# Transposing the attention probabilities with SyncE's DMA queue in place of TensorE, in a fused layer on 8 cores

## Chip, cores and metric

The program runs on 8 NeuronCores of one Trainium2 chip, all with the same instructions and each with its own slice of the tokens; no core waits for another. The metric is the device time in microseconds of the slowest core.

## What is computed

The input is two sequences of 4096 tokens of width 2048. The layer normalizes them, runs local attention (32 heads of 64, blocks of 64 tokens that see their neighbours, and 16 "sink" keys per head) and a feed-forward net of 8192 beside it, and adds their gated product:

```python
xn = _layernorm(x, axis=-1)
# attention: q, k (rotated), v from xn; per head and block of queries
s_band = einsum(Qb, Kband) * scale            # masked to |distance| <= 64
s_sink = einsum(Qb, sinks) * scale
p = softmax(concatenate([s_sink, s_band], -1))
O = p[..., :S] @ sinks + p[..., S:] @ Vband
s = O @ Wo.T + bo
g = silu((silu(gate) * up) @ w_down.T)        # gate, up from xn
x = x + s * g
```

## The kernel before

Each core owns 1024 tokens and 64 more on either side, 1152 in all. The program has four stages, with a barrier between them: the layer norm with its transposes (up to about 150 us), the merged stage of projections and attention (about 150 to 1250 us), the feed-forward net with the output projection (to about 2900 us), and the last transposes with the residual. Only the merged stage is touched.

**The merged stage.** It has 17 steps. Step c (0 to 15) makes the projections of chunk c, which is two heads: two units of q and three of k (two of 512 tokens, one of 128), 16 matmuls each (L513), and where c is even nine units of v for the next four heads (L526 to L529). In the same step the attention of the chunk before, c-1, is done: eight *pairs* j, one for each 128 queries. Units and pairs alternate in the queue of every engine: unit, pair, unit, pair, until one kind runs out. So an odd step has five units and eight pairs, an even step (2 to 14) fourteen units and eight pairs, and step 16 has eight pairs alone. In an odd step the last three or four pairs stand with no unit between them; this text calls them the *tail*. Pairs 16 to 23 belong to step 3 and pairs 24 to 31 to step 4.

**A pair.** For each of two heads (A and B), 128 queries against 256 keys and 16 sinks:

1. `sc` on TensorE: masks, sinks and keys into `psA`, `psB` (L545 to L548).
2. `mx` on VectorE: the two row maxima, scaled (L632 to L636).
3. `ex` on ScalarE: the exponentials into `pA_bf`, `pB_bf`, 128x272 bf16 (L693, L696).
4. `nm` on VectorE: reciprocal of the sums and two scalings in place (L641 to L646). L646 is its last instruction.
5. `tp` on TensorE: six transposes into `ps_tp` (L557 to L562), four of 128x128 for the keys and two for the 16 sinks.
6. `ev` on VectorE: four copies, two of 128x256 to `pt_sb` (L651, L652) and two of 16x128 to `pts_sb` (L653, L654).
7. `av` on TensorE: the product with v, six matmuls into `ps_o` (L577 to L583).
8. `oe` on ScalarE: two copies to `o_buf` (L663, L665).

**What sets the order.** The lists `tsched`, `vsched` and `ssched` are built once (L403 to L437) and every engine follows its list in order. For pair j TensorE has sc(j), tp(j-1), av(j-2); VectorE mx(j), nm(j), ev(j-1); ScalarE ex(j), oe(j-2). What is left at a step's end, av of the last but one pair, tp and av of the last, is put ahead of the next step's units on TensorE. `pA_bf`, `pB_bf`, `pt_sb` and `pts_sb` have two buffers each, by j modulo 2; `ps_tp` and `ps_o` have one. Semaphores count in the order of the lists. A unit of q or k needs, after its matmuls, L619 on VectorE, four copies on ScalarE (L679 to L682), then L623 and L627 on VectorE.

**Queues.** GpSimd issues the weight loads (`pm_gp`, three buffers `wx`, each load when the load three before has been used up). SyncE issues one DMA a chunk, `o_buf` to DRAM (`pm_sync`, L703), and has no other work in this stage.

Of the kernel before, what the change touches and what calls it, by code (L numbers as in the profile page):

```python
# [8 lines left out]
BF16 = mybir.dt.bfloat16  # L9
# [78 lines left out]
def build_program2():  # L88
# [32 lines left out]
    with ExitStack() as glob:  # L121
# [149 lines left out]
        with ExitStack() as sA:  # L271
# [279 lines left out]
            def p3_emit_tp(t, i):  # L551
                ctx.wait(t, "VS", vs_nm[i])
                if i >= 1:
                    ctx.wait(t, "VS", vs_pt[i - 1])
                pt = ps_tp
                pa, pb = pA_bf[i % 2], pB_bf[i % 2]
                t.transpose(pt[:, 0:128], pa[:, NS:NS + 128], id_bf[:])  # L557
                t.transpose(pt[:, 128:256], pa[:, NS + 128:NS + 256], id_bf[:])
                t.transpose(pt[0:NS, 256:384], pa[:, 0:NS], id_bf[:])
                t.transpose(pt[:, 384:512], pb[:, NS:NS + 128], id_bf[:])  # L560
                t.transpose(pt[:, 512:640], pb[:, NS + 128:NS + 256], id_bf[:])
                ins = t.transpose(pt[0:NS, 640:768], pb[:, 0:NS], id_bf[:])  # L562
                ctx.inc(ins, "TS")

            def p3_emit_av(t, i):
                c, qt = pairs[i]
                ctx.wait(t, "VS", vs_pt[i])
                if i >= 1:
                    ctx.wait(t, "SS", ss_oe[i - 1])
                vu = [u for u in unit_of_step[2 * (c // 2)] if u[0] == "v"][-1]  # L570
                ctx.wait(t, "SS", ss_sw[unit_idx[vu]])
                for hh in range(2):
                    h = 2 * c + hh
                    co = hh * 256
                    tp_ = (0, 0) if hh == 0 else (0, 64)
                    outp = ps_o[0:64, :] if hh == 0 else ps_o[64:128, :]
                    t.matmul(outp, v_t[:, qt, h * 64:(h + 1) * 64],  # L577
                             pt_sb[i % 2][:, co:co + 128], start=True, stop=False,
                             tile_position=tp_)
                    t.matmul(outp, v_t[:, qt + 1, h * 64:(h + 1) * 64],  # L580
                             pt_sb[i % 2][:, co + 128:co + 256], start=False, stop=False,
                             tile_position=tp_)
                    ins = t.matmul(outp, sinkn_bf[:, h * 64:(h + 1) * 64],  # L583
                                   pts_sb[i % 2][:, hh * 128:hh * 128 + 128],
                                   start=False, stop=True, tile_position=tp_)
                ctx.inc(ins, "TS")
# [14 lines left out]
            def pm_vector(v):  # L601
                TB.wait_all(v)
                for kind, x in vsched:
                    if kind == "u":
                        u = units[x]
                        i = x
                        _, oc, tsi, off, ln, li = u
                        p = ps_qk[i % 2]
                        sw = t2sw[i % 2]
                        ctx.wait(v, "TS", ts_mm[i])  # L610
                        if oc < 16:
                            cs, ss_ = (ck_t[:, HALO + off:HALO + off + ln],
                                       sk_t[:, HALO + off:HALO + off + ln])
                            dst = q_f[:, oc, off:off + ln]
                        else:
                            cs, ss_ = (ck_t[:, off:off + ln],
                                       sk_t[:, off:off + ln])
                            dst = k_f[:, oc - 16, off:off + ln]
                        ctx.inc(v.scalar_tensor_tensor(  # L619
                            t1[:, 0:ln], p[:, 0:ln], bq_pc[:, oc:oc + 1], cs,  # L620
                            OP.add, OP.mult), "VS")
                        ctx.wait(v, "SS", ss_sw[i])
                        v.scalar_tensor_tensor(  # L623
                            m2[:, 0:ln], sw[:, 0:ln], bq_sw[:, oc:oc + 1], ss_,
                            OP.add, OP.mult)
                        v.drain()
                        ctx.inc(v.tensor_add(dst, t1[:, 0:ln], m2[:, 0:ln]), "VS")  # L627
                        v.drain()
                    elif kind == "mx":
                        j = x  # L630
                        ctx.wait(v, "TS", ts_sc[j])
                        v.reduce_max(nmA[j % 2][:], psA[j % 2][:], axis=AX, negate=True)  # L632
                        v.reduce_max(nmB[j % 2][:], psB[j % 2][:], axis=AX, negate=True)
                        v.drain()
                        v.tensor_mul(n2A[j % 2][:], nmA[j % 2][:], consts[:, 3:4])
                        ctx.inc(v.tensor_mul(n2B[j % 2][:], nmB[j % 2][:],  # L636
                                             consts[:, 3:4]), "VS")
                    elif kind == "nm":
                        j = x
                        ctx.wait(v, "SS", ss_ex[j])  # L640
                        v.reciprocal(rcA[j % 2][:], rsA[j % 2][:])  # L641
                        v.reciprocal(rcB[j % 2][:], rsB[j % 2][:])
                        v.drain()
                        v.tensor_scalar_mul(pA_bf[j % 2][:], pA_bf[j % 2][:],
                                            rcA[j % 2][:])
                        ctx.inc(v.tensor_scalar_mul(pB_bf[j % 2][:], pB_bf[j % 2][:],  # L646
                                                    rcB[j % 2][:]), "VS")
                    else:
                        j = x
                        ctx.wait(v, "TS", ts_tp[j])  # L650
                        v.tensor_copy(pt_sb[j % 2][:, 0:256], ps_tp[:, 0:256])  # L651
                        v.tensor_copy(pt_sb[j % 2][:, 256:512], ps_tp[:, 384:640])  # L652
                        v.tensor_copy(pts_sb[j % 2][:, 0:128], ps_tp[0:NS, 256:384])  # L653
                        ctx.inc(v.tensor_copy(pts_sb[j % 2][:, 128:256],  # L654
                                              ps_tp[0:NS, 640:768]), "VS")

            def pm_scalar(sc):
                def emit_oevac(i):
# [9 lines left out]
                for kind, x in ssched:  # L668
# [19 lines left out]
                    elif kind == "ex":  # L688
                        j = x
                        ctx.wait(sc, "VS", vs_mx[j])  # L690
                        if j >= 2:
                            ctx.wait(sc, "TS", ts_tp[j - 2])
                        sc.activation(pA_bf[j % 2][:], psA[j % 2][:], AF.Exp,  # L693
                                      bias=n2A[j % 2][:], scale=consts[:, 3:4],
                                      accum_out=rsA[j % 2][:])
                        ctx.inc(sc.activation(pB_bf[j % 2][:], psB[j % 2][:],  # L696
                                              AF.Exp, bias=n2B[j % 2][:],
                                              scale=consts[:, 3:4],
                                              accum_out=rsB[j % 2][:]), "SS")
                    else:  # L700
                        emit_oevac(x)

            def pm_sync(s):  # L703
                for c in range(16):
                    last_i = c * NT_OWN + (NT_OWN - 1)
                    ctx.wait(s, "SS", ss_oe[last_i])
                    tok = OS.dma(s, d_oscr[c], o_buf[c % 2][:], c % 2)
                    assert tok == ostok[c]

            with ExitStack() as sPM:  # L710
                ps_qk = [sPM.enter_context(nc.psum_tensor(f"ps_qk{i}", [128, 512], F32))
                         for i in range(2)]
                psA = [sPM.enter_context(nc.psum_tensor(f"psA{i}", [128, 272], F32))
                       for i in range(2)]
                psB = [sPM.enter_context(nc.psum_tensor(f"psB{i}", [128, 272], F32))
                       for i in range(2)]
                ps_tp = sPM.enter_context(nc.psum_tensor("ps_tp", [128, 768], BF16))
                ps_o = sPM.enter_context(nc.psum_tensor("ps_o", [128, 128], F32))
                block.tensor(pm_tensor)
                block.vector(pm_vector)  # L720
                block.scalar(pm_scalar)
                block.sync(pm_sync)
                assert ctx.cnt["TS"] == cTS and ctx.cnt["VS"] == cVS
                assert ctx.cnt["SS"] == cSS
# [440 lines left out]
```

## Time and profile before

| | us |
|---|---|
| runs of the kernel before | 2919.94 and 3130.13, median 3025.03 |
| profiled execution, its own time | 2927.64 |
| its span on the slowest core (core 0) | 2926.0 |
| spans of the 8 cores | 2887.6 to 2926.0 |
| merged stage on core 0 | about 150 to 1250 |

The trace is that of core 0 in the profiled execution. A busy time sums the instructions of one engine; the granted clock is TensorE's, as a share of full speed. TensorE is busy 83% of the span, VectorE 28%, ScalarE 19%. The profiled execution's own time is 1.6 us above its span.

### The profile page before, as it was taken

Reading aid. Unit: us, or ns where it says so; the run is one execution under the profiler, and the core shown is the slowest. Engines: PE = TensorE matmul, PEld = TensorE weight load, DVE = VectorE, ACT = ScalarE, POOL = GpSimd, SP = SyncE. Lnnn points to the kernel's source line nnn. Section 1 sums busy time; section 2 is a strip of 40 time slices with the busy share of each in tenths; the row PEclk is TensorE's granted clock in tenths of the full one; section 3 lists DMA queues with packets and bytes.
Section 4 is the critical chain, followed back from the end, with each engine's and each line's share of the span. In section 5 each row is a group of like instructions: output and inputs, shape, how many; then the busy total and the mean of one; then the engine's idle time right before and its main releaser. Section 6 shows DMA issues by size and latency. Waiting matters only on the chain.

```text
span 2926.0 us, 33018 instructions; the slowest of 8 cores (2887.6 to 2926.0 us)
## 1 busy us (share of the span) xinstructions
PE 2421.4 (83%) x11736; PEld 1129.6 (39%) x11736; DVE 824.2 (28%) x2481; ACT 547.8 (19%) x1351; POOL 136.8 (5%) x259
## 2 busy tenths in 40 slices
PE   2377777878787878779999999999999999997775
PEld 1143343434343434334444444444444444442223
DVE  5234343343434343501302112131211213021114
ACT  4133333333333333400000000000000000000000
POOL 0000000000000000001010010100001010000000
PEclk9977777878686868589999999999999999998885
DMA  4420101011111110067154361614526152442216
GB/s 131 63 37 19 33 19 33 19 37 24 29 25 33 26 26 12 5 133 123 22 87 72 60 113 31 111 33 79 93 52 122 26 99 49 74 85 36 36 34 225
DMA packets 50749, 173.03 MB, mean 59 GB/s; under 512 B 10144, under 2 KB 11296, under 8 KB 46368
## 3 DMA queue, kind: packets, MB, share of 16 engines
q0 software_dynamic: 41616, 135.03, 27.4%
q1 hardware_dynamic: 8976, 35.90, 3.8%
q8 instruction: 100, 1.64, 0.2%
q14 instruction: 57, 0.47, 0.0%
HBM read 293.34 MB, written 12.58 MB: 105 GB/s over the span
## 4 chain that ended last, share of the span: by engine, by line
PE 61%; DMA 12%; DVE 11%; ACT 8%; issue 5%; DVEq 2%; POOL 1%; SPq 0%; ACTq 0%; POOLq 0%
PE ps_d L877 15%; PE ps_g L851 12%; PE ps_u L863 12%; DMA wd_ib<-wd_pack 7%; PE ps_qk L526 5%; PE ps_s L892 5%; PE ps_qk L513 4%; DMA wobuf<-wo_pack 3%; ACT pB_bf L696 2%; ACT pA_bf L693 2%; DVE m L623 1%; DVE t L619 1%; DVE nmA L632 1%; PE ps_o L577 1%; PE ps_o L583 1%
## 5 line engine op out<-in xcount | busy, mean ns | idle before, releaser
L877 PE MATMUL ps_d<-h_ib,wd_ib 128*128 128x512 bf16 x2048 | 458.2, 386 | 38.3 <-DMA wd_ib<-wd_pack 38.3
L851 PE MATMUL ps_g<-xn_f,gbuf 128*128 128x512 bf16 x2048 | 464.5, 380 | 15.1 <-DMA gbuf<-wgu_pack 15.1
L863 PE MATMUL ps_u<-xn_f,ubuf 128*128 128x512 bf16 x2048 | 462.9, 379 | 0.0
L513 PE MATMUL ps_qk<-xn_f,wx 128*128 128x512 bf16 (+1 forms) x1280 | 313.8, 411 | 34.6 <-DMA wx<-wqkv_pack 28.8
L929 DVE TENSOR_TENSOR h_ib<-tg,ps_u 128x512 bf16<-128x512 f32 x128 | 88.1, 688 | 815.8 <-PE ps_u L863 815.8
L877 PEld LDWEIGHTS ps_d<-h_ib,wd_ib 128*128 128x128 bf16 x2048 | 202.8, 99 | 291.0 <-issue 58.4
L907 ACT ACTIVATE tg<-ps_g 128x512 f32<-128x512 f32 x128 | 76.4, 597 | 1238.7 <-PE ps_g L851 1238.7
L851 PEld LDWEIGHTS ps_g<-xn_f,gbuf 128*128 128x128 bf16 x2048 | 200.7, 98 | 257.8 <-issue 17.4
L863 PEld LDWEIGHTS ps_u<-xn_f,ubuf 128*128 128x128 bf16 x2048 | 200.4, 98 | 241.6
L939 DVE TENSOR_TENSOR g_sb<-g_sb,ps_d 128x512 f32<-128x512 f32 x224 | 154.0, 688 | 273.6 <-PE ps_d L877 273.6
L557 PE MATMUL ps_tp<-id_bf,pA_bf 128*128 128x128 bf16 x128 | 31.9, 249 | 212.5 <-DVE pts_sb L654 157.4
L513 PEld LDWEIGHTS ps_qk<-xn_f,wx 128*128 128x128 bf16 x1280 | 128.9, 113 | 194.2 <-issue 114.6
L892 PE MATMUL ps_s<-o_sb,wobuf 128*128 128x512 bf16 x512 | 143.4, 450 | 61.3 <-DMA wobuf<-wo_pack 61.3
L526 PE MATMUL ps_qk<-wx,xn_f 128*128 128x256 bf16 x1152 | 158.3, 297 | 4.0 <-DVE k_f L627 4.0
L693 ACT ACTIVATE pA_bf<-psA,n2A,consts_sb 128x272 bf16<-128x272 f32 x128 | 73.9, 577 | 326.7 <-DVE n2B L636 271.7
L526 PEld LDWEIGHTS ps_qk<-wx,xn_f 128*128 128x128 bf16 x1152 | 115.3, 105 | 32.3 <-issue 4.1
L892 PEld LDWEIGHTS ps_s<-o_sb,wobuf 128*128 128x128 bf16 x512 | 56.3, 112 | 148.3 <-issue 109.1
L623 DVE SCALAR_TENSOR_TENSOR m<-t2sw,bq_sw,sk_t 128x512 f32<-128x512 f32 (+1 forms) x80 | 53.7, 671 | 187.0 <-ACT t2sw L682 187.0
L557 PEld LDWEIGHTS ps_tp<-id_bf,pA_bf 128*128 128x128 bf16 x128 | 12.8, 100 | 236.2 <-issue 232.5
L577 PE MATMUL ps_o<-pt_sb,v_t 128*64 128x128 bf16 x256 | 71.8, 280 | 36.6 <-DVE pts_sb L654 36.6
L619 DVE SCALAR_TENSOR_TENSOR t<-ps_qk,bq_pc,ck_t 128x512 f32<-128x512 f32 (+1 forms) x80 | 52.6, 657 | 145.1 <-PE ps_qk L513 144.4
L37 POOL DMA_DIRECT2D gbuf<-wgu_pack x64 | 33.9, 530 | 1170.8 <-PE ps_g L851 1027.1
(93 smaller groups left out, 2001.6 us busy)
## 6 DMA issues: line engine op xcount, KB each, us to landing
gbuf<-wgu_pack POOLq DMA_DIRECT2D x64, 512.0 KB, 5.5
ubuf<-wgu_pack POOLq DMA_DIRECT2D x64, 512.0 KB, 5.8
wd_ib<-wd_pack POOLq DMA_DIRECT2D x64, 512.0 KB, 18.3
wx<-wqkv_pack POOLq DMA_DIRECT2D x32, 512.0 KB, 5.1
u_all<-u_ext SPq DMA_DIRECT2D x9, 1024.0 KB, 18.2
wx<-v_pack POOLq DMA_DIRECT2D x8, 1024.0 KB, 9.1
wobuf<-wo_pack POOLq DMA_DIRECT2D x16, 512.0 KB, 5.0
u_buf<-u_ext SPq DMA_DIRECT2D x8, 1024.0 KB, 7.7
```

What stands on the lines that cost most here:

```text
L513: ins = t.matmul(p[:, 0:ln], w[:, kc * 128:(kc + 1) * 128], src[:, kc, :], start=(kc == 0), stop=(kc == 15))
L526: t.matmul(p[:, 0:256], xn_f[:, kc, tt * 128:(tt + 1) * 128], w[:, kc * 256:(kc + 1) * 256], start=(kc == 0), stop=False)
L577: t.matmul(outp, v_t[:, qt, h * 64:(h + 1) * 64], pt_sb[i % 2][:, co:co + 128], start=True, stop=False, tile_position=tp_)
L619: ctx.inc(v.scalar_tensor_tensor(t1[:, 0:ln], p[:, 0:ln], bq_pc[:, oc:oc + 1], cs, OP.add, OP.mult), "VS")
L623: v.scalar_tensor_tensor(m2[:, 0:ln], sw[:, 0:ln], bq_sw[:, oc:oc + 1], ss_, OP.add, OP.mult)
L693: sc.activation(pA_bf[j % 2][:], psA[j % 2][:], AF.Exp, bias=n2A[j % 2][:], scale=consts[:, 3:4], accum_out=rsA[j % 2][:])
L851: ins = t.matmul(pg[:], gbuf[ic % 2][:, kc * 128:(kc + 1) * 128], xn_f[:, kc, HALO + tsx * 512:HALO + (tsx + 1) * 512], start=(kc == 0), s ...
L863: ins = t.matmul(pu[:], ubuf[ic % 2][:, kc * 128:(kc + 1) * 128], xn_f[:, kc, HALO + tsx * 512:HALO + (tsx + 1) * 512], start=(kc == 0), s ...
L877: ins = t.matmul(pd[:], wd_ib[:, ic, oc * 128:(oc + 1) * 128], h_ib[:, ic, tsx * 512:(tsx + 1) * 512], start=(ic == 0), stop=(ic == 7))
L892: ins = t.matmul(pw[:], wobuf[0][:, kc * 128:(kc + 1) * 128], o_sb[:, kc, tw * 512:(tw + 1) * 512], start=(kc == 0), stop=(kc == 15))
L929: ctx.inc(v.tensor_mul(h_ib[:, ic, tsx * 512:(tsx + 1) * 512], tg[gi % 2][:], ps_u[gi % 2][:]), "VS")
L939: ins = v.tensor_add(dst, dst, ps_d[j % 2][:])
```

## The change

The four transposes of the keys' probabilities leave TensorE. SyncE issues four DMA transposes for each pair instead, from `pA_bf` and `pB_bf` in SBUF straight to `pt_sb` in SBUF, 128x128 bf16 each, 512 of them in the stage. The two small transposes of the sinks stay on TensorE, with `ps_tp` cut to 16x256, and their two copies on VectorE; the two large copies L651 and L652 go. SyncE waits for nm(j), and for av(j-2), which has read the same `pt_sb`. av(j) waits for the four transposes of its pair (semaphore `pt`, 64 counts), and so does ex(j+2), which writes over `pA_bf` and `pB_bf`. The DMA of `o_buf` stands in the same queue of SyncE, behind the transposes of the chunk's last pair, and waits for oe of that pair.

```diff
@@ -554,17 +554,14 @@
                     ctx.wait(t, "VS", vs_pt[i - 1])
                 pt = ps_tp
                 pa, pb = pA_bf[i % 2], pB_bf[i % 2]
-                t.transpose(pt[:, 0:128], pa[:, NS:NS + 128], id_bf[:])
-                t.transpose(pt[:, 128:256], pa[:, NS + 128:NS + 256], id_bf[:])
-                t.transpose(pt[0:NS, 256:384], pa[:, 0:NS], id_bf[:])
-                t.transpose(pt[:, 384:512], pb[:, NS:NS + 128], id_bf[:])
-                t.transpose(pt[:, 512:640], pb[:, NS + 128:NS + 256], id_bf[:])
-                ins = t.transpose(pt[0:NS, 640:768], pb[:, 0:NS], id_bf[:])
+                t.transpose(pt[:, 0:128], pa[:, 0:NS], id_bf[:])
+                ins = t.transpose(pt[:, 128:256], pb[:, 0:NS], id_bf[:])
                 ctx.inc(ins, "TS")
 
             def p3_emit_av(t, i):
                 c, qt = pairs[i]
                 ctx.wait(t, "VS", vs_pt[i])
+                PT.wait(t, pttok[i])
                 if i >= 1:
                     ctx.wait(t, "SS", ss_oe[i - 1])
                 vu = [u for u in unit_of_step[2 * (c // 2)] if u[0] == "v"][-1]
@@ -648,11 +645,9 @@
                     else:
                         j = x
                         ctx.wait(v, "TS", ts_tp[j])
-                        v.tensor_copy(pt_sb[j % 2][:, 0:256], ps_tp[:, 0:256])
-                        v.tensor_copy(pt_sb[j % 2][:, 256:512], ps_tp[:, 384:640])
-                        v.tensor_copy(pts_sb[j % 2][:, 0:128], ps_tp[0:NS, 256:384])
+                        v.tensor_copy(pts_sb[j % 2][:, 0:128], ps_tp[:, 0:128])
                         ctx.inc(v.tensor_copy(pts_sb[j % 2][:, 128:256],
-                                              ps_tp[0:NS, 640:768]), "VS")
+                                              ps_tp[:, 128:256]), "VS")
 
             def pm_scalar(sc):
                 def emit_oevac(i):
@@ -690,6 +685,7 @@
                         ctx.wait(sc, "VS", vs_mx[j])
                         if j >= 2:
                             ctx.wait(sc, "TS", ts_tp[j - 2])
+                            PT.wait(sc, pttok[j - 2])
                         sc.activation(pA_bf[j % 2][:], psA[j % 2][:], AF.Exp,
                                       bias=n2A[j % 2][:], scale=consts[:, 3:4],
                                       accum_out=rsA[j % 2][:])
@@ -700,12 +696,34 @@
                     else:
                         emit_oevac(x)
 
+            PT = Slots(nc, glob, "pt", 2)
+            pttok = [None] * NP3
+            ptc = [0, 0]
+            for j in range(NP3):
+                ptc[j % 2] += 64
+                pttok[j] = (j % 2, ptc[j % 2])
+
             def pm_sync(s):
-                for c in range(16):
-                    last_i = c * NT_OWN + (NT_OWN - 1)
-                    ctx.wait(s, "SS", ss_oe[last_i])
-                    tok = OS.dma(s, d_oscr[c], o_buf[c % 2][:], c % 2)
-                    assert tok == ostok[c]
+                for j in range(NP3):
+                    c, qt = pairs[j]
+                    ctx.wait(s, "VS", vs_nm[j])
+                    if j >= 2:
+                        ctx.wait(s, "TS", ts_av[j - 2])
+                    pa, pb = pA_bf[j % 2], pB_bf[j % 2]
+                    dst = pt_sb[j % 2]
+                    s.dma_start_transpose(dst[:, 0:128],
+                                          pa[:, NS:NS + 128]).then_inc(PT.sems[j % 2], 16)
+                    s.dma_start_transpose(dst[:, 128:256],
+                                          pa[:, NS + 128:NS + 256]).then_inc(PT.sems[j % 2], 16)
+                    s.dma_start_transpose(dst[:, 256:384],
+                                          pb[:, NS:NS + 128]).then_inc(PT.sems[j % 2], 16)
+                    s.dma_start_transpose(dst[:, 384:512],
+                                          pb[:, NS + 128:NS + 256]).then_inc(PT.sems[j % 2], 16)
+                    PT.cnt[j % 2] += 64
+                    if qt == NT_OWN - 1:
+                        ctx.wait(s, "SS", ss_oe[j])
+                        tok = OS.dma(s, d_oscr[c], o_buf[c % 2][:], c % 2)
+                        assert tok == ostok[c]
 
             with ExitStack() as sPM:
                 ps_qk = [sPM.enter_context(nc.psum_tensor(f"ps_qk{i}", [128, 512], F32))
@@ -714,7 +732,7 @@
                        for i in range(2)]
                 psB = [sPM.enter_context(nc.psum_tensor(f"psB{i}", [128, 272], F32))
                        for i in range(2)]
-                ps_tp = sPM.enter_context(nc.psum_tensor("ps_tp", [128, 768], BF16))
+                ps_tp = sPM.enter_context(nc.psum_tensor("ps_tp", [NS, 256], BF16))
                 ps_o = sPM.enter_context(nc.psum_tensor("ps_o", [128, 128], F32))
                 block.tensor(pm_tensor)
                 block.vector(pm_vector)
```

TensorE at tp and av of one pair of step 1, before (the number behind a buffer's name is its index; VS and SS are VectorE's and ScalarE's counts):

```order
L557 MATMUL ps_tp<-id_bf,pA_bf1 128x128 [waits VS]
L558 MATMUL ps_tp<-id_bf,pA_bf1 128x128
L559 MATMUL ps_tp<-id_bf,pA_bf1 16x128
L560 MATMUL ps_tp<-id_bf,pB_bf1 128x128
L561 MATMUL ps_tp<-id_bf,pB_bf1 128x128
L562 MATMUL ps_tp<-id_bf,pB_bf1 16x128
L577 MATMUL ps_o<-pt_sb0,v_t 64x128 [waits VS,SS]
L580 MATMUL ps_o<-pt_sb0,v_t 64x128
```

The same place now (`pt0` is the semaphore of the DMA transposes into `pt_sb0`):

```order
L557 MATMUL ps_tp<-id_bf,pA_bf1 16x128 [waits VS]
L558 MATMUL ps_tp<-id_bf,pB_bf1 16x128
L574 MATMUL ps_o<-pt_sb0,v_t 64x128 [waits VS,pt0,SS]
L577 MATMUL ps_o<-pt_sb0,v_t 64x128
L580 MATMUL ps_o<-pts_sb0,sinkn_bf 64x128
```

Four matmuls have gone from between the two places, and the first matmul of av has one more wait, with everything behind it in TensorE's queue.

SyncE at the end of chunk 0, now (before, its queue held only the DMA of `o_buf` here, once a chunk):

```order
L714 DMA_TRANSPOSE pt_sb1<-pA_bf1 128x128 [waits VS,TS]
L716 DMA_TRANSPOSE pt_sb1<-pA_bf1 128x128
L718 DMA_TRANSPOSE pt_sb1<-pB_bf1 128x128
L720 DMA_TRANSPOSE pt_sb1<-pB_bf1 128x128
L37 DMA o_scr<-o_buf0 128x1024 [waits SS]
L714 DMA_TRANSPOSE pt_sb0<-pA_bf0 128x128 [waits VS,TS]
```

The queue has four transposes a pair, all in one line, and the store of a chunk lies between two pairs.

## Rows read from the trace of the kernel before

**Rows 1.** Windows, core 0: attention stage, a tail, a v stretch; columns in the header row.
```profile
core 0: us, PE busy (x) PEld busy (x) DVE busy (x) ACT busy (x) POOL busy (x), PEclk, DMA share, GB/s
150.00:1250.00 1100.00, 848.99 (x4728) 424.01 (x4728) 446.97 (x1765) 401.24 (x1144) 18.49 (x35) 0.76 0.13 25
351.00:371.00 20.00, 13.58 (x69) 5.77 (x69) 9.69 (x52) 7.51 (x26) 0.00 (x0) 0.50 0.00 0
431.00:446.00 15.00, 15.00 (x122) 10.82 (x121) 3.19 (x17) 3.95 (x12) 0.00 (x0) 1.00 0.01 1
```

**Rows 2.** Waits of 150 to 1250 us: us in total, times, longest.
```profile
DVE rcA L641 <- ACT pB_bf L696: 189.8, 128, 1.8
...
PE ps_tp L557 <- DVE pts_sb L654: 157.4, 75, 5.9
```

**Rows 3.** Timeline of DVE, projection-paced pairs 16 and 17: start us, us, work.
```profile
321.14 0.28 DVE L646 TENSOR_SCALAR pB_bf<-pB_bf,rcB 128x272 bf16<-128x272 bf16 x1
...
329.37 0.28 DVE L646 TENSOR_SCALAR pB_bf<-pB_bf,rcB 128x272 bf16<-128x272 bf16 x1
329.57 0.28 DVE L651 COPY pt_sb<-ps_tp 128x256 bf16<-128x256 bf16 x1
329.77 0.28 DVE L652 COPY pt_sb<-ps_tp 128x256 bf16<-128x256 bf16 x1
```

**Rows 4.** Timeline of DVE, tail: the last scaling of pairs 19, 20, 21, 23.
```profile
347.24 0.28 DVE L646 TENSOR_SCALAR pB_bf<-pB_bf,rcB 128x272 bf16<-128x272 bf16 x1
...
353.70 0.28 DVE L646 TENSOR_SCALAR pB_bf<-pB_bf,rcB 128x272 bf16<-128x272 bf16 x1
...
357.61 0.28 DVE L646 TENSOR_SCALAR pB_bf<-pB_bf,rcB 128x272 bf16<-128x272 bf16 x1
...
365.55 0.28 DVE L646 TENSOR_SCALAR pB_bf<-pB_bf,rcB 128x272 bf16<-128x272 bf16 x1
```

**Rows 5.** Timeline of PE: tp of pair 15, start of av of pairs 16, 19, 23.
```profile
304.90 0.23 PE L557 MATMUL ps_tp<-id_bf,pA_bf 128*128 128x128 bf16 x1
...
305.49 0.22 PE L562 MATMUL ps_tp<-id_bf,pB_bf 128*16 128x128 bf16 x1
...
331.18 0.24 PE L577 MATMUL ps_o<-pt_sb,v_t 128*64 128x128 bf16 x1
...
355.82 0.32 PE L577 MATMUL ps_o<-pt_sb,v_t 128*64 128x128 bf16 x1
...
370.34 0.28 PE L577 MATMUL ps_o<-pt_sb,v_t 128*64 128x128 bf16 x1 [1.20 <-DVE pts_sb L654]
```

**Rows 6.** Timelines of DVE and PE: pair 24, pair 31 and the last eight pairs.
```profile
385.59 0.28 DVE L646 TENSOR_SCALAR pB_bf<-pB_bf,rcB 128x272 bf16<-128x272 bf16 x1
...
...
448.86 0.22 PE L577 MATMUL ps_o<-pt_sb,v_t 128*64 128x128 bf16 x1 [1.20 <-DVE pts_sb L654]
...
1215.59 0.28 DVE L646 TENSOR_SCALAR pB_bf<-pB_bf,rcB 128x272 bf16<-128x272 bf16 x1
...
1247.50 0.29 PE L577 MATMUL ps_o<-pt_sb,v_t 128*64 128x128 bf16 x1 [1.24 <-DVE pts_sb L654]
```

**Rows 7.** DMA of 300 to 1250 us: queue share; issues by count, KB, us to landing.
```profile
q0 software_dynamic: 4320, 18.88, 11.4%
...
wx<-wqkv_pack POOLq DMA_DIRECT2D x24, 512.0 KB, 5.1
wx<-v_pack POOLq DMA_DIRECT2D x6, 1024.0 KB, 8.9
o_scr<-o_buf SPq DMA_DIRECT2D x15, 256.0 KB, 2.1
```

**Rows 8.** Timeline of the SyncE and GpSimd queues: the issue of one DMA each.
```profile
308.47 0.33 SPq L37 DMA_DIRECT2D o_scr<-o_buf  x1
...
342.52 0.53 POOL L37 DMA_DIRECT2D wx<-v_pack  x1 [24.08 <-PE ps_qk L513]
```

## Prediction

> **What bounds the kernel now.** I read first the windows of the stage that is touched, then the waits in it, then the timelines of single pairs. In the merged stage TensorE is busy 849 of 1100 us and VectorE 447, and TensorE's granted clock is 0.76 [rows 1]: nothing is full, so chains of waits set the pace. The waits show a loop between VectorE and ScalarE: VectorE waits for the exponentials once a pair, 189.8 us in all, and TensorE waits 157.4 us for the copies that clear `ps_tp` [rows 2]. The timelines then show three regimes.
>
> *Projection-paced pairs* (a q or k unit before each). From one L646 to the next it takes 329.37 - 321.14 = 8.2 us [rows 3]. VectorE does a unit, then mx, nm and ev in a line, with ScalarE between, and ev starts as soon as L646 is done (329.57). So what ev loses comes off the period, while the transposes on TensorE lie in its idle time.
>
> *The tail of an odd step.* No unit is between the pairs, and VectorE's line alone takes 357.61 - 353.70 = 3.9 us [rows 4]. TensorE is busy 13.58 of 20 us there at clock 0.50, the lower level, 1.2 GHz [rows 1].
>
> *The v stretch of an even step.* TensorE is busy 15.00 of 15 us at clock 1.00 [rows 1]: there each matmul that goes is time.
>
> The quantity that decides about the new transfer is the slack from nm(j) to av(j), since it has to land in it. Pair 16 has 331.18 - 321.42 = 9.8 us, pair 19 has 355.82 - 347.52 = 8.3, and pair 23, the last of its tail, 370.34 - 365.83 = 4.5 [rows 3 to 5].
>
> **What goes.** On VectorE, L651 and L652: each holds the engine 0.20 us (329.57 to 329.77 [rows 3]), 0.4 us a pair where its line sets the pace. On TensorE, four of six transposes: the six take 305.71 - 304.90 = 0.8 us at full clock [rows 5], so four are 0.5 us, which count in the v stretch and where a step ends in tp, ev, av with nothing behind them. Elsewhere they go from under a wait.
>
> **What comes.** Four DMA transposes a pair, one behind the other in SyncE's queue. No row shows one. Let p be the time from one issue to the next. The last lands 3p + 2.1 us after nm, taking 2.1 us from issue to landing as for the store of `o_buf` [rows 7]; 0.3 us more pass until TensorE starts. From below p is 0.33 us, what SyncE needs to issue a plain DMA [rows 8]. From above it is 2.1 us, if each has to land before the next begins. The two ends are far apart, and no row is like a transpose, whose pieces are short runs; their middle is 1.2. I take 1.3, a little to the serial side, because all four use the same 16 engines. Then a pair needs 5.2 us of the queue and 3.9 + 2.1 + 0.3 = 6.3 us from nm to av.
>
> The Trainium skill (VectorE: DVE Perf Modes, The three transpose paths) gives 1309 ns for a 128x128 bf16 transpose by DMA and advises TensorE where PSUM will do. That speaks against this change: four would be 5.2 us a pair. The trace has TensorE's transposes 0.13 us apart, and no row for the other. By its figure the sum would be the one below.
>
> Against the slack: 6.3 is under 9.8 and 8.3, so projection-paced pairs hide it. In the tail it doesn't hide: the queue needs 5.2 us a pair where the line took 3.9, and the last pair has 4.5 us of slack.
>
> - *Odd step* (8 of them). The copies of pairs 16 to 19 save 4 x 0.4 = 1.6 us. From nm(20) at 353.98 to av(23) at 370.34 it took 16.4 us [rows 4, 5]. Now 16 transposes go through: 15p + 2.1 + 0.3 = 21.9. Net +5.5 - 1.6 = +3.9 us, or 15p - 15.6 in general.
> - *Even step* (7). Four copies save 1.6. In the v stretch four pairs save 0.5 each, of which I keep 1.5, since 5.2 us a pair is about the pace there. At its end tp and ev lie bare and save 0.5 + 0.4; the transposes of the last pair have long landed, because six v units stand between. Net -4.0 us.
> - *Step 16* (eight pairs, no units). From nm(120) at 1215.87 to av(127) at 1247.50 it took 31.6 us [rows 6]; 32 transposes take 31p + 2.4 = 42.7. Net +11.1 us.
> - *Weight loads on the same engines.* 30 loads hold the engines for 11.4% of 950 us, 3.6 us each [rows 7]. Most meet pairs with slack. The load of v at 342.5 [rows 8], 8.9 us long, meets pair 19, whose margin is 8.3 - 6.3 = 2.0 us, and the queue hands the rest to the tail. I take 1 us for each odd step: +8. At worst it is 3.6 - 2.0 = 1.6 a step, at best 0.
>
> Sum: 8 x 3.9 - 7 x 4.0 + 11.1 + 8 = +22 us. Against the profiled execution's own 2927.6 that gives 2950 us, +0.8%. Of the runs shown, one is just below the profiled time and one far above, and their median of 3025 lies between the two; I forecast for runs like the profiled one. A measurement of this kernel can tell about 2%, 58 us, from no change.
>
> The waits behind the new one: TensorE holds sc of the next pair and, at a step's end, the first unit behind av. ScalarE holds ex(j+2) until pair j has landed, and oe behind it; with two buffers that costs nothing until the queue is the pace. SyncE's store of `o_buf` waits for oe of the last pair, and the next transposes come some 15 us later (nm of pair 23 at 365.8, of 24 at 385.9 [rows 4, 6]).
>
> **Rivals.**
>
> *Cheap transposes (faster).* At p = 0.33 the last lands 3.4 us after nm, inside every slack, and only savings stay. Odd step: seven copies, 2.8 us, and 1.1 at its end, 3.9. Even step: 1.6 + 2.0 + 0.9 = 4.5. Step 16: 3.9. Sum 31 + 32 + 4 = 67, giving 2861 us. It holds nearly so while 4p stays under 3.5 us, p below 0.9; at that end, where the 4.5 us of slack is used up, about 2875. For it: SyncE is idle and the DMA engines are busy 13% [rows 1]. Against it: a transpose turns 128 rows into short pieces.
>
> The Trainium skill (Advanced Engine Details and Errata, X-Bar Transpose (TRN2)) says that such DMAs are as fast as regular ones. The trace has no row for it. By that rule p would be near an issue, and the time this rival's.
>
> *The queue becomes the pace (slower).* If the transposes hardly overlap, the odd step's 15p - 15.6 and step 16's 31p - 29.2 decide. The sum passes 58 us at about p = 1.5. At 1.8 it is 8 x 11.4 - 7 x 3 + 26.6 = +97, or 3025 us. At p = 2.1 the queue needs 8.4 us a pair and sets whole steps: 67.5 us from the first nm to the last av, against 48.9 in an odd step (321.42 to 370.34) and 63.0 in an even one (385.87 to 448.86) [rows 3, 5, 6]; 8 x 18.6 + 7 x 4.5 + 35.9 = +216, or 3144 us. For it: the serial end is a real row's landing time, and each transpose has its own completion.
>
> *Interleaving with weight loads (slower).* If a load's 3.6 us falls wholly on the path twice in a pair of steps, 2 x 3.6 x 7.5 = 54 us come on top of the forecast less its 8: 2996 us. It decides only if loads meet tails, and the one at 342.5 ends just before; so I hold it for less likely.
>
> **How the numbers follow.** Forecast 0.42; cheap transposes 0.20; queue as pace 0.25; interleaving 0.13. Faster by over 2% (under 2869) takes half of the cheap case, 0.10. Within 2% are the forecast and the other half, 0.52. Slower is the rest, 0.38. The range runs from 2868, near the end of the cheap case, to 3110, short of the fully serial end. The forecast's own range, p from 1.0 to 1.5, is about 2900 to 2985.
>
> **What would show it.** SyncE's issues of DMA transposes and their landings give p. Right: tails at about 5.2 us from the last scaling of one pair to that of the next, in place of 3.9; av waiting for DMA in tails and hardly in projection-paced pairs, whose period falls from 8.2 to 7.8; even steps shorter, step 16 longer by some 11 us. Wrong: waits for the transposes in every pair, the stage's clock clearly off 0.76, or p outside 1.0 to 1.5.

## The result, and the profile after

The changed kernel takes 2973 us in the median of 14 runs against 2947 of 13 runs of the kernel before; the ratio is 1.0101, 95% interval 1.0057 to 1.0145. The medians take in executions in which the cores of one die or both ran at a lower clock (the kernel before took up to 3144 us in them); the ratio compares the others. It is +30 us, with 17 to 43 inside the interval: slower, by more than the measurement is uncertain, and less than the 2% (58 us) that the prediction took for the least that can be told from no change. The stated range holds it. The forecast was +22 us and "within 2%" as the likeliest case. The absolute 2950 was too low by 23 us mostly because it stood on a profiled execution that was itself 19 us under the median of before.

Under this total lie two parts that don't agree with it as neatly. The span of the attention work, from the first scaling (nm of pair 0) to av of pair 127, read from the timelines of all eight cores, went from 1064.1 to 1110.3 us in the mean: +46, twice the forecast. The feed-forward stage took 6 us less in that execution, in the mean of the cores. On single cores the first took 1062 to 1065 us before and 1104 to 1119 after, the second 1554 to 1584 and 1541 to 1596. In the mean of three profiles of each kernel the attention span grew by 43 us.

**The page after**, engines and slices (core 4, the slowest):

```profile
PE 2328.5 (78%) x11058; PEld 1090.5 (37%) x11224; DVE 775.0 (26%) x2225; ACT 548.8 (18%) x1351; POOL 137.3 (5%) x259
...
PE   2476676757576758559999999999999999997775
...
DVE  5233333333333333311312112131211203121114
...
PEclk9977787878787868679999999999999999998885
```

TensorE and VectorE are less busy than before, by 93 and 49 us (the page before is that of core 0), and the kernel is slower: the busy time of the whole was not the limit. The figure of TensorE is a little low, since some matmul records are missing from this trace. The chain of work that ended last shows where the time went; before, then after:

```profile
PE 61%; DMA 12%; DVE 11%; ACT 8%; issue 5%; DVEq 2%; POOL 1%; SPq 0%; ACTq 0%; POOLq 0%
```

```profile
PE 53%; DMA 15%; SPq 9%; DVE 8%; ACT 7%; issue 5%; POOL 1%; DVEq 1%; ACTq 0%; POOLq 0%
```

SyncE's queue (SPq), which was not on it, now holds 9% of the span.

The waits of 150 to 1300 us on core 0 (engine, line, who was waited for: us in total, times, longest), to set beside [rows 2]:

```profile
DVE rcA L638 <- ACT pB_bf L692: 224.4, 128, 3.5
...
PE ps_o L574 <- DMA pt_sb<-pB_bf: 154.0, 60, 4.7
PE ps_tp L557 <- DVE pts_sb L649: 141.8, 58, 5.9
...
ACT pA_bf L689 <- DMA pt_sb<-pB_bf: 90.2, 31, 4.1
```

TensorE waits 154.0 us for the transposes, in 60 of 128 pairs, which is new; the last pair of all, just past 1300 us, adds 4.6. ScalarE waits another 90.2 us for them, for its buffers. The wait at tp for VectorE's copies hardly changed (157.4 to 141.8), though these copies were halved.

SyncE's queue in the tail of step 3 (start us, us, instruction), pairs 20 and 21 with the first of pair 22:

```profile
362.87 1.09 SPq L714 DMA_TRANSPOSE pt_sb<-pA_bf  x1
364.00 2.01 SPq L716 DMA_TRANSPOSE pt_sb<-pA_bf  x1
366.06 1.24 SPq L718 DMA_TRANSPOSE pt_sb<-pB_bf  x1
367.33 1.24 SPq L720 DMA_TRANSPOSE pt_sb<-pB_bf  x1
368.71 1.13 SPq L714 DMA_TRANSPOSE pt_sb<-pA_bf  x1
...
373.82 1.13 SPq L714 DMA_TRANSPOSE pt_sb<-pA_bf  x1
```

From 368.71 to 373.82 the four transposes of pair 21 take 5.1 us, 1.28 from one issue to the next. The one at 364.00 is longer: 33 of the 512 on this core took over 1.4 us, 22 us more in all than they would at 1.23. The DMA view of 300 to 1280 us gives the median landing:

```profile
pt_sb<-pA_bf SPq DMA_TRANSPOSE x220, 2.4
pt_sb<-pB_bf SPq DMA_TRANSPOSE x220, 2.4
```

So p is 1.28 and the landing 2.4 us after issue, where the forecast had 1.3 and 2.1, neither from a row of a transpose. Its 0.3 us from landing to TensorE's start stood in no row at all; where av waited for the transposes, 0.35 us passed in the median.

The last scalings of pairs 19 to 23 on VectorE, which stand to [rows 4]:

```profile
356.35 0.28 DVE L643 TENSOR_SCALAR pB_bf<-pB_bf,rcB 128x272 bf16<-128x272 bf16 x1
...
362.46 0.28 DVE L643 TENSOR_SCALAR pB_bf<-pB_bf,rcB 128x272 bf16<-128x272 bf16 x1
...
366.36 0.28 DVE L643 TENSOR_SCALAR pB_bf<-pB_bf,rcB 128x272 bf16<-128x272 bf16 x1
...
371.65 0.28 DVE L643 TENSOR_SCALAR pB_bf<-pB_bf,rcB 128x272 bf16<-128x272 bf16 x1
...
376.93 0.29 DVE L643 TENSOR_SCALAR pB_bf<-pB_bf,rcB 128x272 bf16<-128x272 bf16 x1
```

The periods are now 6.1, 3.9, 5.3 and 5.3 us where they were 6.5, 3.9, 4.0 and 3.9. The first of the tail still run at VectorE's own pace, until two pairs are in flight and ScalarE has no buffer; then they run at the queue's. Pair 23 has its av here:

```profile
385.36 0.29 PE L574 MATMUL ps_o<-pt_sb,v_t 128*64 128x128 bf16 x1 [3.54 <-DMA pt_sb<-pB_bf]
```

It starts 385.36 - 377.22 = 8.1 us after its scaling, against 4.5 before: it waits in the queue behind pair 22.

### The profile page after: what moved, and what is told of

Read it like the earlier page. It is cut to its first block, busy times and chain, and to the rows that moved or that the text cites. A ratio compares the mean times of both kernels' runs of the same rounds, so it can differ in the third digit from the quotient of the medians.

```text
span 2979.6 us, 32592 instructions; the slowest of 8 cores (2917.9 to 2979.6 us)
## 1 busy us (share of the span) xinstructions
PE 2328.5 (78%) x11058; PEld 1090.5 (37%) x11224; DVE 775.0 (26%) x2225; ACT 548.8 (18%) x1351; POOL 137.3 (5%) x259
## 4 chain that ended last, share of the span: by engine, by line
PE 53%; DMA 15%; SPq 9%; DVE 8%; ACT 7%; issue 5%; POOL 1%; DVEq 1%; ACTq 0%; POOLq 0%
PE ps_d L895 14%; PE ps_g L869 11%; PE ps_u L881 11%; DMA wd_ib<-wd_pack 8%; PE ps_s L910 5%; PE ps_qk L513 4%; PE ps_qk L526 4%; DMA pt_sb<-pB_bf 3%; DMA wobuf<-wo_pack 3%; SPq L718 2%; SPq L716 2%; SPq L714 2%; SPq L720 2%; ACT pB_bf L692 1%; DVE m L620 1%
## 5 line engine op out<-in xcount | busy, mean ns | idle before, releaser
L557 PE MATMUL ps_tp<-id_bf,pA_bf 128*16 128x128 bf16 x128 | 31.3, 245 | 202.2 <-DVE pts_sb L649 146.1
L574 PEld LDWEIGHTS ps_o<-pt_sb,v_t 128*64 128x64 bf16 x256 | 30.1, 118 | 211.9 <-issue 198.7
L557 PEld LDWEIGHTS ps_tp<-id_bf,pA_bf 128*16 128x16 bf16 x128 | 11.0, 86 | 224.4 <-issue 220.8
```

Of the source, the lines that this page charges most:

```text
L574: t.matmul(outp, v_t[:, qt, h * 64:(h + 1) * 64], pt_sb[i % 2][:, co:co + 128], start=True, stop=False, tile_position=tp_)
```

## Experiments

The table gives the attention span and its parts as means over eight cores, in us. "Odd", "even" and "step 16" run from the first scaling of a step to its last av. The last column is the feed-forward stage, from its first gate matmul to the last matmul of the output projection.

| kernel | span | odd | even | step 16 | feed-forward |
|---|---|---|---|---|---|
| before | 1064.1 | 49.2 | 61.7 | 31.6 | 1567 |
| before2 | 1063.7 | 49.2 | 61.7 | 31.6 | 1587 |
| before3 | 1064.7 | 49.2 | 61.7 | 31.6 | 1555 |
| after | 1110.3 | 54.3 | 60.6 | 42.3 | 1561 |
| after2 | 1106.6 | 53.9 | 60.4 | 42.3 | 1560 |
| after3 | 1104.3 | 53.8 | 60.5 | 42.0 | 1547 |
| none (transposes left out) | 990.8 | 45.8 | 56.2 | 28.3 | 1568 |
| half | 1033.2 | 47.8 | 58.5 | 30.5 | 1560 |
| wide2 | 1006.7 | 47.0 | 56.5 | 29.7 | 1567 |
| wide1 | 994.0 | 45.9 | 56.2 | 29.3 | 1568 |
| wide1b | 993.3 | 46.0 | 56.2 | 29.4 | 1583 |
| buf3 | 1107.6 | 54.0 | 60.7 | 42.3 | 1550 |

**none: what the removed work was worth.** It leaves out all DMA transposes but those of the first two pairs, with their waits.

```diff
-                    s.dma_start_transpose(...)
+                    if j < 2:
+                        s.dma_start_transpose(...)
-                ptc[j % 2] += 64
+                ptc[j % 2] += (64 if j < 2 else 0)
```

> The changed kernel without its DMA transposes, all but those of the first two pairs: the work is left out, pt_sb keeps old values and nothing waits for them. It prices the saving alone. My sum of the savings (two copies of 0.4 us a pair on VectorE, four transposes of 0.5 us on TensorE in the v stretch): from the first scaling to the last av 67 us less than before's 1064.6, so about 998; even steps -4.5 us each, odd steps -3.9, step 16 -3.9. Rival, that the savings were over-counted: even steps about -1, the whole -40 or less, about 1025. Total time: 2946 - 67 = about 2880 by mine, about 2905 by the rival.

The profiled execution took 2855 us. The span fell by 73.3 us: odd steps -3.4, even steps -5.5, step 16 -3.3. The sum of savings, 67, was right and rather low, but its parts were off both ways: odd steps and step 16 gave less than 3.9, the time between steps 4 us that nobody had counted, and even steps more than 4.5. The reason is visible in the windows of the v stretch, each from nm of a step's fifth pair to av of its eighth (columns as in [rows 1]). First the kernel before, steps 2 and 4:

```profile
279.68:306.92 27.24, 26.04 (x205) 17.50 (x205) 8.54 (x45) 8.96 (x29) 0.53 (x1) 0.98 0.04 5
418.47:448.86 30.39, 29.19 (x204) 18.42 (x204) 8.54 (x45) 8.96 (x29) 0.53 (x1) 0.85 0.04 4
```

It takes 27.2 us at a mean clock of 0.98 and 30.4 at 0.85, with the same 204 or 205 matmuls in both and the same 1.2 us of idle TensorE: three microseconds are the clock's. The lower level (0.50) began before the stretch in both, where TensorE has gaps of 1 to 5.5 us, and reached 0.8 us into the first and 8.8 us into the second. Then none, steps 2 and 4:

```profile
272.48:296.64 24.16, 22.84 (x183) 15.88 (x183) 6.54 (x35) 8.58 (x28) 0.53 (x1) 1.00 0.02 2
401.99:426.15 24.16, 22.91 (x183) 15.88 (x183) 6.54 (x34) 8.58 (x28) 0.53 (x1) 1.00 0.03 3
```

Here the stretch takes 24.2 us at clock 1.00, as in six of the seven even steps. So what the change takes away is worth 3 us in this stretch where the clock was already high, and 6 where it also comes up.

**wide2: half the instructions, the same bytes.**

```diff
-                    s.dma_start_transpose(dst[:, 0:128], pa[:, NS:NS + 128])
-                    s.dma_start_transpose(dst[:, 128:256], pa[:, NS + 128:NS + 256])
+                    s.dma_start_transpose(
+                        dst[:, 0:256].rearrange("p (a b) -> p a b", a=2),
+                        pa[:, NS:NS + 256])
```

and the same for `pb`.

> Two DMA transposes a pair, 128x256 each, in place of four of 128x128; same bytes. If the price is one of each instruction (1.27 us from issue to issue whatever its width), the queue needs 2.5 us a pair, the last lands about 4 us after the scaling and everything is hidden: stage about 1064.6 - 60 = 1005, tails at 3.5 us a pair, total about 2885 to 2895. If the price goes with the bytes or the 16x128 blocks (a 128x256 one takes 2.5 us), nothing changes: stage about 1115, odd steps +5 us against before, total about 2975.

The span is 1006.7 us, 104 less than with four; the ratio to before is 0.981, interval 0.972 to 0.990. The price is one of each instruction: 1.17 and 1.25 us for twice the columns, with an odd long one here too.

```profile
351.95 2.11 SPq L717 DMA_TRANSPOSE pt_sb<-pB_bf  x1
354.31 1.17 SPq L714 DMA_TRANSPOSE pt_sb<-pA_bf  x1
355.52 1.25 SPq L717 DMA_TRANSPOSE pt_sb<-pB_bf  x1
```

**half: head A by DMA, head B on TensorE.**

```diff
+                t.transpose(pt[:, 0:128], pb[:, NS:NS + 128], id_bf[:])
+                t.transpose(pt[:, 128:256], pb[:, NS + 128:NS + 256], id_bf[:])
...
+                        v.tensor_copy(pt_sb[j % 2][:, 256:512], ps_tp[:, 0:256])
```

> Head A by two DMA transposes, head B on TensorE with one wide copy on VectorE, as before. The queue needs 2.5 us a pair. If the queue's pace in the tails and in step 16 is what makes the changed kernel slower: tails fall below 3.9 us a pair (about 3.7), odd steps about -2 us against before, step 16 about -2, stage about 1040, total about 2925. If it is the wait itself (issue to landing 2.4 us, the loads beside it, or ScalarE held by the new wait) the odd steps stay at +2 or more and the stage above 1080.

Odd steps -1.4 us, step 16 -1.1, span 1033.2, ratio 0.992 (0.987 to 0.998). The new wait and the landing of 2.4 us are all there, and nothing is lost. With two instructions a pair the queue takes 2.5 us against VectorE's line of 3.9. So the wait itself is not what cost. (The expected 2 us an odd step were 1.4; its tails ran at 3.8 us a pair.)

**buf3: is it the buffer or the queue?** The same change is made to `pB_bf` and `pt_sb`. ScalarE's 90.2 us of waits made the buffers a rival to the queue's pace, since ex(j+2) may not overwrite what pair j's transposes still read.

```diff
-            pA_bf = [... for i in range(2)]
+            pA_bf = [... for i in range(3)]
-                        if j >= 2:
-                            PT.wait(sc, pttok[j - 2])
+                        if j >= 3:
+                            PT.wait(sc, pttok[j - 3])
```

> The changed kernel with three buffers in place of two for pA_bf, pB_bf and pt_sb (the row of ones is cut to the 128 values that are used, to make room). ScalarE's exponentials then wait for the transposes three pairs back and not two, and SyncE for av three pairs back. If the pace of SyncE's queue (4 x 1.27 = 5.1 us a pair) makes the loss, nothing moves: odd steps stay at +5 us against before, step 16 at +12, stage 1112 to 1117. If ScalarE's wait for the buffer (89.5 us in the profile) makes it, the tails fall towards 3.9 us a pair and the stage by 15 us or more.

Odd steps 54.0, step 16 42.3, span 1107.6: as the changed kernel in its second profile (the expected 1112 to 1117 stood on cores 0 and 4 of the first). The buffers only chose where the queue's pace was waited for.

**before2 and after2: what repeats.**

> The kernel before once more, unchanged, for how far its stages vary from one execution to the next. In the two profiles the merged stage grew by some 45 to 53 us while the total grew by 30; the feed-forward stage took 1554 to 1584 us on the 8 cores before and 1541 to 1595 after. If that is chance, the feed-forward stage here differs by 10 to 20 us from the first profile of the same kernel on single cores and the merged stage by under 3. If the change shortens it, both stages repeat to a few us on every core.

> The changed kernel once more, unchanged. The merged stage repeated to 0.1 us between two profiles of the kernel before, while the feed-forward stage moved by 10 to 45 us on single cores. So here the merged stage should be 1112 to 1117 us from the first scaling to the last av on each core, +47 to +52 against before, and the ratio of times should move from 1.010 towards 1.016, which is what the merged stage alone would give. If the change shortens the feed-forward stage instead, its mean over the cores stays at 1560 against 1567 and 1587 in the two profiles of before, and the ratio stays at 1.010.

The attention span of before repeated to 0.4 us in the mean (to 3.5 on single cores), that of after to 4. The feed-forward stage, untouched, moved by 20 us in the mean of the kernel before. after2 missed its expectation of 1112 to 1117 us on each core: the cores took 1101 to 1112, so the first profile was on the long side. Its ratio is 1.0123 (1.0078 to 1.0168), which lies inside the first interval and the first inside its own; 1.016 is inside too.

**before3 and after3: does the change shorten the feed-forward stage?**

> The kernel before, a third profile. The feed-forward stage took a mean of 1567 and 1587 us over the 8 cores in its two profiles, and 1561 and 1560 in the two of the changed kernel. If the difference of 17 us is chance, this one may fall on either side of 1565; if the changed kernel's feed-forward stage is truly shorter (its cores leave the merged stage 20 us apart, not 8, and load the same weights), it is again at 1567 or above. The merged stage is 1064 us.

> The changed kernel, a third profile. Mean of the feed-forward stage over the cores: under 1565 if it is truly shorter than before's, else anywhere from 1555 to 1590. Merged stage 1105 to 1112 us in the mean.

The attention spans are 1064.7 and 1104.3 us in the mean; the latter is just under the expected 1105 to 1112, and the three profiles of the changed kernel span 6 us, those of before 1. The feed-forward means are 1555 us (before3) and 1547 (after3): the kernel before fell on the other side, and below both earlier profiles of the changed one. Three profiles each give 1567, 1587, 1555 and 1561, 1560, 1547. Over the profiles of all versions, twelve of them, it lies between 1547 and 1587. The changed kernel's three lie in the low half, with 14 us between the means, which is less than the spread of either. Whether the change gives a few microseconds back there stays open; the runs neither show it nor rule it out.

**wide1 and wide1b: one transpose a pair.** `pA_bf` and `pB_bf` become the two halves of one tensor of 544 columns. In the scores of head B the sinks stand behind the keys, so that columns 16 to 528 are the keys of both heads. This changes the score matmuls of head B a little too: its sinks no longer pass through the mask.

```diff
+            pAB = [ea(nc.sbuf_tensor(f"pAB{i}", [128, 544], BF16)) for i in range(2)]
+                    s.dma_start_transpose(
+                        dst[:].rearrange("p (a b) -> p a b", a=4),
+                        pAB[j % 2][:, NS:NS + 512])
...
+                        t.matmul(ps[:, 256:272], qsl, sinkt_bf[...], start=True, stop=True)
+                        t.matmul(ps[:, 0:256], id_bf[:], masks_bf[:, qt, NS:272],
+                                 start=True, stop=False)
```

> One DMA transpose a pair, 128x512: A and B lie side by side in one tensor, with B's sinks behind its keys, so that the 512 key columns are contiguous. In the profile of two a pair the price was 1.24 us of each instruction at twice the width. If it stays one price of each (the last lands 2.4 us after the scaling), no pair waits and the time is that of the kernel with the transposes left out: stage 991 to 997 us against 1003 with two a pair, tails 3.5 us a pair, total about 20 us under two a pair's low ones, 2850 to 2875. If the price grows with the width from here (2.5 us or more), the stage stays at 1000 to 1005 and the total at about 2875.

> One DMA transpose of 128x512 a pair, once more and with more timed rounds, since its ratio of 0.983 had an interval of 0.9755 to 0.990. Its merged stage was 70 us shorter than before's, which alone would give 0.976. Expected 0.976 to 0.983, and clearly below 0.99.

The span is 994.0 us (993.3 in wide1b), 3 above the kernel that does no transposes. The ratio is 0.983 (0.976 to 0.990) and, with more runs, 0.981 (0.976 to 0.986). One transpose of 128x512 holds the queue no longer than one of 128x128, and TensorE's waits for them are down from 154.0 us to 10.1. The transpose of one pair, and the waits:

```profile
349.92 1.19 SPq L722 DMA_TRANSPOSE pt_sb<-pAB  x1
```

```profile
PE ps_o L582 <- DMA pt_sb<-pAB: 10.1, 5, 2.5
```

wide1 beats the kernel before by 1.9%, and the changed one by about 3% (0.981 / 1.010 = 0.971). wide2 reached the same ratio within the intervals; in the attention span wide1 is 13 us better.

## Why the prediction was right or wrong

**The mechanism was right where it cost most, and so was the sign of the sum; one term failed, that of the even steps (below).** The forecast had the queue's pace in the tails and in step 16, slack elsewhere. On core 0 TensorE waits for the transposes in all four tail pairs of each odd step and in all of step 16, as it said. buf3 and half single the pace out against the two other readings of the same waits, the buffer and the wait itself.

**The price p, 1.3 against 1.28: right, by luck as much as by reason.** It was taken near the middle of 0.33 and 2.1 us, because the profile had no row. The sum depends on little else: a tenth of a microsecond more adds about 15 us (from 15p in eight steps and 31p in one). The figure of the Trainium skill (VectorE: DVE Perf Modes, The three transpose paths), 1309 ns for 128x128 by DMA, agrees with the 1.28 us of this trace from one issue to the next, not with the 2.4 to the landing. The Trainium skill (VectorE: DVE Perf Modes, Rules for kernel authors) advises TensorE where PSUM will do. This holds here for four transposes a pair and fails for one (ratio 0.981).

**The landing, 2.1 against 2.4:** a small miss; half and wide2 have the same landing and lose nothing.

**Odd steps:** forecast +3.9 and 1 more for the loads, measured +5.1. Right in the sum; inside it the first pairs saved 0.7 and not 1.6 (below), and the tail, from nm(20) to av(23) in the mean 22.1 us against 16.4, lost 5.7 and not 6.5. The two misses cancel, which is luck.

**Step 16:** forecast +11.1, measured +10.7. Right.

**Even steps: this step failed.** Forecast -4.0 each, measured -1.1; seven of them are 20 of the 24 us by which the span grew more than forecast (8 x 5.1 - 7 x 1.1 + 10.7 = 43.8, and 2 between the steps). none shows that the savings themselves are there, 5.5 us, so the transposes take 4.4 back, and the forecast had allowed 0.5: it kept 1.5 of 2.0 us because 5.2 us a pair "is about the pace there". The slack from nm to av, which it called the quantity that decides, it never read for the pairs of this stretch. The fifth pair is the one that matters. Here are its last scaling and its av in step 4, first in none, then in the changed kernel with its last transpose:

```profile
401.70 0.29 DVE L643 TENSOR_SCALAR pB_bf<-pB_bf,rcB 128x272 bf16<-128x272 bf16 x1
...
406.79 0.24 PE L574 MATMUL ps_o<-pt_sb,v_t 128*64 128x128 bf16 x1
```

```profile
431.53 0.28 DVE L643 TENSOR_SCALAR pB_bf<-pB_bf,rcB 128x272 bf16<-128x272 bf16 x1
...
436.27 1.24 SPq L720 DMA_TRANSPOSE pt_sb<-pB_bf  x1
...
439.00 0.22 PE L574 MATMUL ps_o<-pt_sb,v_t 128*64 128x128 bf16 x1 [2.31 <-DMA pt_sb<-pB_bf]
```

Over all cores and even steps this slack was 8.5 us before. Once the savings are in (none) it is 5.2, since TensorE reaches the av sooner. Four transposes take 7.2 there, so av waits, about 2 us in each even step on core 0.

That wait seems to have a second price, the clock. These are windows of step 4 in the changed kernel (columns as in [rows 1]):

```profile
433.00:441.00 8.00, 5.68 (x46) 3.85 (x46) 3.07 (x18) 3.78 (x13) 0.00 (x0) 0.98 0.13 29
441.00:451.00 10.00, 10.00 (x47) 5.45 (x46) 2.10 (x11) 2.43 (x8) 0.00 (x0) 0.50 0.13 26
451.00:456.00 5.00, 5.00 (x44) 3.89 (x42) 0.00 (x0) 0.77 (x2) 0.00 (x0) 1.00 0.09 18
```

TensorE waits 2.3 us up to 439.00, and from 441 to 451 it is busy without a gap at clock 0.50, the lower level: 47 matmuls in 10 us, against 44 in the 5 us after them. The clock falls inside the stretch in 53 of 56 stretches (seven on each of eight cores) of the changed kernel, in 8 of 56 in none and in none of 56 before. Since none differs from the changed kernel in the transposes alone, it is they that bring the fall; that it is their wait is read from the order in time. The whole stretch in steps 4 and 6 of the changed kernel, to set beside those of before and none above:

```profile
431.81:462.48 30.67, 27.16 (x183) 17.48 (x183) 6.56 (x35) 8.67 (x28) 0.53 (x1) 0.83 0.11 20
577.40:604.90 27.50, 24.93 (x187) 16.85 (x187) 6.55 (x34) 9.10 (x29) 0.53 (x1) 0.94 0.11 22
```

In the mean of all cores and even steps:

| | stretch | TensorE busy | TensorE idle | clock |
|---|---|---|---|---|
| before | 29.0 | 27.8 | 1.2 | 0.91 |
| none | 24.5 | 23.1 | 1.3 | 0.99 |
| after | 28.9 | 25.5 | 3.4 | 0.90 |

Against before, TensorE's work fell by 2.3 us, about the 2.5 that the forecast took off for it. Its idle time grew by 2.2, where the forecast had 0.5 for the transposes less 0.4 for the copies: this is the mis-sized term. Against none, 2.1 of the 4.4 us are idle time and 2.4 are longer matmuls, so the forecast also missed a gain of the clock that the change would have had, and that the wait took away. Why the lower level of before, which starts ahead of the stretch, lasts longer than that of none (17.0 against 6.9 us in step 4) stays open.

**The first pairs of a step:** forecast -1.6 (four copies of 0.4), measured -1.0. Between nm of a step's first pair and nm of its fifth lie only three evs, since ev(j-1) stands behind nm(j): in none the first period is as before (8.3 us) and the next three are each 0.3 to 0.4 us shorter, so the 8.2 of [rows 3] did not become 7.8. A counting error, 0.6 us in each of 15 steps. (In the odd steps of the changed kernel only 0.7 us is left of it, as the fourth period is 6.5 us where it is 6.2 in none.)

**Rivals.** Cheap transposes: their premise, a spacing near the 0.33 us of a plain issue, did not hold, it was 1.28. The time given, 2861 us, is nearly what wide1 and wide2 reach, at a price of 1.2 us but once or twice a pair. What decides is the number of instructions, a variable that the prediction held fixed. (Its bound was also miscounted: at p = 0.9 the last would land 3 x 0.9 + 2.4 = 5.1 us after nm, past the 4.5 of slack, which is used up at 0.7.) The queue as the pace of whole steps: not reached, since p stayed under the 1.5 from which it would have decided.

Interleaving with weight loads: it happens, and costs nothing where it falls. In 7 of 8 odd steps on core 0 the third pair's last transpose is in flight with the load of v and lands 6.4 to 9.6 us after issue in place of 2.4; its av waits 3 us on average. Pair 18:

```profile
351.29 0.53 POOL L37 DMA_DIRECT2D wx<-v_pack  x1 [23.29 <-PE ps_qk L513]
...
351.84 1.23 SPq L720 DMA_TRANSPOSE pt_sb<-pB_bf  x1
...
360.51 0.28 PE L574 MATMUL ps_o<-pt_sb,v_t 128*64 128x128 bf16 x1 [3.11 <-DMA pt_sb<-pB_bf]
```

But this pair is projection-paced: from the scaling of the pair before to its own it takes 8.6 us and from there to the next 8.7, as in none. What the same landing would do in a tail no run shows. The forecast had the meeting right, but for pair 19 in place of 18, and its 1 us for each odd step is not seen: 15 x 1.28 + 2.4 + 0.35 = 21.9 us is nearly all of the tail's 22.1.

## What to carry to other kernels

Moving work off a busy engine pays by what stood on the chain of waits, not by the busy time it frees; and the new carrier has a pace of its own that has to be set against the shortest period in the schedule, not the mean one. Read the slack where the schedule is tightest, and as it will be with the savings in: here it shrank from 8.5 to 5.2 us. A DMA transpose cost by the instruction here, up to 128x512: lay the data out so that one instruction takes all of it, before judging whether DMA or TensorE should transpose. Split a small change of the total by stage: a stage that repeats to a few microseconds tells within one or two profiles what the total, with a stage that moves by 20 us, tells in ten runs.

## What was not expected of the hardware

- The time that one DMA transpose held SyncE's queue did not depend on its width: 1.23 us at 128x128, 1.24 at 128x256, 1.19 at 128x512 (medians), source and target in SBUF; the landing was 2.3 to 2.4 us after issue in the median for all three.
- Some transposes held the queue longer, up to 2.6 us, 33 of 512 on core 0 and 42 on core 4; what singles them out was not tested. Those in flight together with the 1024 KB load of v landed up to 9.6 us after issue on core 0.
- Short waits of TensorE in a stretch that it otherwise fills went with a lower clock: in 44 of the 56 stretches of the changed kernel it waited over 1 us (to 3.7) for the transposes, and in 42 of these the granted clock fell from 1.00 to 0.50 within 8 us after the wait began. In all it fell in 53 of 56, and without the transposes in 8 of 56.
- The same stretch of work, 205 matmuls with 1.2 us of idle TensorE, took 27.2 us in one step and 30.4 in another of one profile, at mean granted clocks of 0.98 and 0.85, as the lower level, begun before it, reached 0.8 or 8.8 us into it; with the transposes left out, or with one a pair (wide1, 24.1 us), it ran at 1.00 in six steps of seven.
